# Rope products behind the score maxima on VectorE, and their sum behind the norm of the probabilities on GpSimd

## The reference

```python
q_c = layernorm(x) @ W_dq;  kv_c = ctx @ W_kvc
q_nope, q_rope = q_c @ W_uq, rope(q_c @ W_qr)          # 16 heads of 128 and of 64
k_nope, v, k_rope = kv_c @ W_uk, kv_c @ W_uv, rope(kv_c @ W_kr)
scores = (q_nope . k_nope + q_rope . k_rope) / sqrt(192)
scores = where(key in [seg - 8, seg], scores, -1e30)
x = x + (softmax(scores) @ v) @ W_o
# then: layernorm, gate, the two best of 8 experts per token, mean of their relu outputs, added to x
# rope(x): [x1 * cos - x2 * sin, x1 * sin + x2 * cos]
```

## Time and profile before

| | |
|---|---|
| median of 3 runs | 398.65 us (397.29 to 399.25) |
| the profiled execution | 397.97 us, span from the first to the last instruction 396.0 us |
| busy in the span: TensorE, VectorE, ScalarE, GpSimd | 84%, 69%, 63%, 58% |
| mean granted clock of TensorE | 0.984 |

### The profile page before, as it was taken

The page is one execution under the profiler, slowest core; times in us unless marked ns, Lnnn a source line. Parts: engine busy times, 40 slices in busy tenths (PEclk is TensorE's granted clock), DMA queues, the critical chain, the costliest instruction groups (busy, mean ns, idle before and its releaser), DMA issues.

```text
span 396.0 us, 9935 instructions
## 1 busy us (share of the span) xinstructions
PE 333.5 (84%) x2451; PEld 277.1 (70%) x2451; DVE 274.9 (69%) x1299; ACT 247.5 (63%) x843; POOL 227.8 (58%) x287
## 2 busy tenths in 40 slices
PE   0868999999879898988989898898988988799870
PEld 0656778777667777776777777777766767799750
DVE  2164878577688767778876877887677668756266
ACT  1232866888876777677677767767778635456440
POOL 4067646466975757576576757657655414677700
PEclk9999899999999999999999999999999999999995
DMA  8962711126121212132121213212221025566178
GB/s 288 343 250 83 266 55 55 55 71 171 55 81 56 81 61 99 53 103 83 53 80 67 92 53 106 80 53 80 80 82 54 2 68 156 173 198 190 50 256 293
DMA packets 28788, 45.29 MB, mean 114 GB/s; under 512 B 4428, under 2 KB 20191, under 8 KB 28112
## 3 DMA queue, kind: packets, MB, share of 16 engines
q1 hardware_dynamic: 25104, 37.30, 28.8%
q0 software_dynamic: 2960, 6.94, 4.9%
q10 hardware_dynamic: 688, 0.64, 0.6%
HBM read 26.46 MB, written 19.30 MB: 116 GB/s over the span
## 4 chain that ended last, share of the span: by engine, by line
issue 26%; PE 24%; POOL 23%; DVE 14%; DMA 5%; ACT 4%; POOLq 2%; DVEq 1%; ACTq 0%
POOL prob L1401 9%; PE psum L1163 4%; POOL slots L1421 4%; PE psum L681 3%; PE psum L1149 3%; PE psum L683 3%; PE psum L682 3%; DMA wcat<-in_w_kvc 2%; DVE nsc L1696 2%; POOL rope_c L1396 2%; DMA halves<-jout,jidx 2%; ACT prob L1257 2%; DVE x_all L1577 2%; POOL m_after L1378 1%; POOL mask L1386 1%
## 5 line engine op out<-in xcount | busy, mean ns | idle before, releaser
L1257 ACT ACTIVATE prob<-nsc,nmax 128x128 f32<-128x128 f32 x256 | 100.7, 395 | 62.7 <-DVE nmax L1696 62.7
L1401 POOL TENSOR_TENSOR prob<-prob,prec 128x512 f32<-128x512 f32 x64 | 67.2, 1050 | 27.3 <-DVE prec L1678 27.1
L1396 POOL TENSOR_TENSOR rope_c<-rope_c,rope_s 128x512 f32<-128x512 f32 x32 | 42.0, 1313 | 58.4 <-DVE rope_s L1672 58.3
L1696 DVE CUSTOM_DVE_ANT_0 nsc<-psum,mask 128x128 f32<-128x128 f32 x256 | 58.7, 285 | 18.7 <-PE psum L1163 13.3
L1163 PE MATMUL psum<-kT_all,qT 128*128 (+1 forms) x512 | 67.7, 275 | 1.2 <-DMA qT<-turned 1.2
L1163 PEld LDWEIGHTS psum<-kT_all,qT 128*128 128x128 f32 x512 | 62.2, 192 | 1.4 <-DMA qT<-turned 1.4
L1149 PE MATMUL psum<-ident,prob 128*128 128x128 f32 x256 | 41.8, 286 | 22.3 <-POOL prob L1401 22.3
L1149 PEld LDWEIGHTS psum<-ident,prob 128*128 128x128 f32 x256 | 26.9, 140 | 44.2 <-POOL prob L1401 36.3
L1257 ACT ACTIVATION_READ_ACCUMULATOR prob<-nsc,nmax 128x1 f32 x256 | 48.2, 188 | 0.0
L681 PE MATMUL psum<-qc_hi,wq_hi 96*128 96x256 f32 x128 | 41.6, 325 | 2.2 <-ACT qT L1300 0.9
L1443 POOL DMA_INDIRECT halves<-jout,jidx x33 | 32.8, 994 | 17.0 <-issue 6.8
(11 more groups left out here) (204 smaller groups left out, 821.1 us busy)
## 6 DMA issues: line engine op xcount, KB each, us to landing
turned<-rope_c SPq DMA_DIRECT2D x32, 256.0 KB, 2.0
qT<-turned SPq DMA_DIRECT2D x64, 128.0 KB, 2.4
wanted<-slots SPq DMA_DIRECT2D x33, 129.0 KB, 2.4
wo_raw<-in_w_o SPq DMA_DIRECT2D x2, 1024.0 KB, 15.9
we_raw<-in_expert_w SPq DMA_DIRECT2D x1, 2048.0 KB, 7.8
half<-halves SPq DMA_DIRECT2D x4, 512.0 KB, 7.1
x_all<-in_x SPq DMA_DIRECT2D x2, 640.0 KB, 18.4
slots<-pad_row SPq DMA_DIRECT2D x8, 129.0 KB, 3.7
```

The source lines that it names most:

```text
L1257: e = act.activation(prob[r][:, h, :], nsc[r][:, h, :], ACT.Exp, bias=nmax[r][:, h:h + 1], scale=-1.0, accum_out=psum_h[r][:, h:h + 1])
L1396: pool.tensor_tensor(into[:], into[:], rope_s[:], ALU.add).then_inc(m["rope_joined"], 1)
L1401: pool.tensor_tensor(p[:], p[:], prec[1 - r][:, :].unsqueeze(2).to_broadcast([P, HG, P]), ALU.mult).then_inc(m["prob_normed"], 1)
L1696: e = dve.tensor_tensor_reduce(nsc[r][:, h, :], B_S[r][:, h, :], mask[t][:], -SCALE, BIG, ALU.add, ALU.min, nmax[r][:, h:h + 1])
```

## The change

In even slots VectorE issues the two rope products, with their waits, behind the score maxima of the slot and no longer ahead of the reciprocal; GpSimd issues the norm of the probabilities first and the sum of the rope parts behind it. Nothing else moves, and no instruction is added or left out.

```diff
@@ GpSimd, slot(b, k)
+                if live(i - 1, GROUPS):
+
+                    at_least(pool, "recip_done", i)
+                    p = prob[1 - r]
+                    pool.tensor_tensor(p[:], p[:], prec[1 - r][:, :].unsqueeze(2).to_broadcast([P, HG, P]),
+                                       ALU.mult).then_inc(m["prob_normed"], 1)
                 if k % TPB == 0 and live(pn, QUADS):
                     into = rope_c[(k // TPB) % 2]
                     at_least(pool, "rope_parts", pn + 1)
                     pool.tensor_tensor(into[:], into[:], rope_s[:], ALU.add).then_inc(m["rope_joined"], 1)
-                if live(i - 1, GROUPS):
-
-                    at_least(pool, "recip_done", i)
-                    p = prob[1 - r]
-                    pool.tensor_tensor(p[:], p[:], prec[1 - r][:, :].unsqueeze(2).to_broadcast([P, HG, P]),
-                                       ALU.mult).then_inc(m["prob_normed"], 1)
@@ VectorE, slot(b, k), ahead of the reciprocal
-                if t == 0 and live(p + 2, QUADS):
-
-                    into = (k // TPB) % 2
-                    if isinstance(i, int) and i == -4:
-                        dve.wait_ge(S("ld_ropeq"), 16)
-                    at_least(dve, "qr_done", p + 3)
-                    at_least(dve, f"qr_out{into}", 16 * ((SLOTS // TPB // 2) * b + (k // TPB + 2) // 2))
-                    at_least(dve, "rope_joined", p + 2)
-                    a = B_R.rearrange("p (a n) -> p a n", a=2)
-                    dve.tensor_tensor(rope_c[into][:], a, ropeT[:, 0:1, :].to_broadcast([P, 2, L]), ALU.mult)
-                    dve.tensor_tensor(rope_s[:], a[:, ::-1, :], ropeT[:, 1:3, :], ALU.mult).then_inc(m["rope_parts"], 1)
...
@@ VectorE, slot(b, k), behind the score maxima
+                if t == 0 and live(p + 2, QUADS):
...
+                    dve.tensor_tensor(rope_c[into][:], a, ropeT[:, 0:1, :].to_broadcast([P, 2, L]), ALU.mult)
+                    dve.tensor_tensor(rope_s[:], a[:, ::-1, :], ropeT[:, 1:3, :], ALU.mult).then_inc(m["rope_parts"], 1)
```

More of the change, by code:

```diff
@@ L1392, in slot @@
                 nb, kn = b + k // SLOTS, k % SLOTS
[L1393 to L1396, removed]
                 if live(i - 1, GROUPS):
@@ L1402, in slot @@
                                        ALU.mult).then_inc(m["prob_normed"], 1)
+                if k % TPB == 0 and live(pn, QUADS):
+                    into = rope_c[(k // TPB) % 2]
+                    at_least(pool, "rope_parts", pn + 1)
+                    pool.tensor_tensor(into[:], into[:], rope_s[:], ALU.add).then_inc(m["rope_joined"], 1)
                 if kn == 0 and live(nb, B):
@@ L1699, in slot @@
                             e.then_inc(m["score_max"], 1)
+                if t == 0 and live(p + 2, QUADS):
+                    into = (k // TPB) % 2
+                    if isinstance(i, int) and i == -4:
+                        dve.wait_ge(S("ld_ropeq"), 16)
+                    at_least(dve, "qr_done", p + 3)
+                    at_least(dve, f"qr_out{into}", 16 * ((SLOTS // TPB // 2) * b + (k // TPB + 2) // 2))
+                    at_least(dve, "rope_joined", p + 2)
+                    a = B_R.rearrange("p (a n) -> p a n", a=2)
+                    dve.tensor_tensor(rope_c[into][:], a, ropeT[:, 0:1, :].to_broadcast([P, 2, L]), ALU.mult)
+                    dve.tensor_tensor(rope_s[:], a[:, ::-1, :], ropeT[:, 1:3, :], ALU.mult).then_inc(m["rope_parts"], 1)
                 if step == 1 and live(w, TILES) and not (isinstance(i, int) and i >= GROUPS):
```

## The result

The changed kernel takes 443.89 us (440.96 to 444.54, 4 runs) against 398.95 us (397.29 to 400.3, 4 runs): 1.1114 times the time before, 95% interval 1.1047 to 1.1181, or 44.9 us more. That is slower, as forecast, and 0.9 us above the upper end of the range (443). The profiled execution took 443.3 us; its span is 441.5 us.

What follows compares the result with a forecast made beforehand. GpSimd's order in slots with indirect DMAs (0, 1, 4, 5) was taken to set when TensorE's next slot opens. Waits of 27.5 us and 9.5 us of clock on 397.97, plus 0.7 for the median, gave 435 us, range 420 to 443.

Steps and rivals of the forecast that it cites:

- GpSimd's queue: Slots 0 and 4: mask, row copy, DMAs and next norm queue behind the sum waiting for late products; +2.13 and +2.21 us.
- Slots 0 to 2: Loop batch: the late sum delays mask, DMAs and slot 1's norm, so slot 2 opens 2.13 us later.
- slots 4 to 6: Loop batch: same delay on GpSimd, with no mask; slot 6 opens 2.21 us later.
- slots 2 to 4: VectorE: products now precede batch_sum, so slot 4 opens 0.62 us later, bounds 0 and 0.62.
- the 26.3 summed: Waits of batches with indirect DMAs, slot 0 six times, slot 4 five times: 6 x 2.75 + 5 x 1.96 us.
- the price of a low stretch: TensorE at 1.2 GHz behind the long waits before slots 2 and 6: 1.2 us each, between 0 and 1.5, eleven times.
- 3.7 hidden: Behind slot 2 the later TensorE hides VectorE's 0.62 us delay of batch_sum: -3.7 us in total.
- The rival whose clock holds (426): The loop's waits grow but TensorE's clock does not fall: 426 us at the median, chance 0.28.
- batches 0 and 1 at 0: Batches without indirect DMAs, where TensorE's own work is longer: no loss, between -1 and +1 us.
- the very first slot at 1.2: Products delay the key rows, for which TensorE waits until 37.30: 1.2 us, between 0 and 1.2.
- Faster: Rival: early norm removes the odd slots' waits, 1.18 us a batch; 391.5 us, chance 0.04.
- Moves nothing: Rival: slot 1's norm is not what TensorE needs next, so the delay lies in slack; 398.65 us, chance 0.03.

Runs made afterwards that it cites:

- warm: Changed kernel plus 13 unread TensorE products of 512 columns at the end of slots 1 and 5, from slot 16 on: 428.91 us, ratio 1.0762 to the kernel before.
- early_to12: The whole change only in slots before 12, the order of the kernel before from there on: 401.53 us, ratio 1.0101.
- early_only: The whole change only in slots before 16, the order of the kernel before from there on: 403.13 us, ratio 1.0149.
- late_only: The whole change only from slot 16 on, the order of the kernel before ahead of that: 439.75 us, ratio 1.1055.
- pool_only: Kernel before with only GpSimd's swap (norm first, rope sum second), VectorE's products in their old place: 397.29 us, ratio 0.9983.
- sum_next: Kernel before with GpSimd's rope sum moved behind the norm of the following odd slot, products in their old place: 389.18 us, ratio 0.9797.
- behind_recip: Changed kernel with VectorE's products directly behind the reciprocal, ahead of xT_lo and the score maxima: 401.82 us, ratio 1.0097 to the kernel before.
- dve_only: Kernel before with only VectorE's products moved behind the score maxima, GpSimd in the old order (sum, then norm): 510.57 us, ratio 1.2818.

## Why the prediction was right and where it was wrong

**GpSimd's queue: right.** Slots 0 to 2 were to grow by 2.13 us and grew by 2.05 (11.69 against 9.64 before); slots 4 to 6 by 2.21, and grew by 2.12 (11.17 against 9.05). The idle time before the sum is named after the products, and the odd slots no longer wait, as the prediction said. For slots 2 to 4 it gave 0.62, the place of batch_sum behind the products: with the clock held, in `warm`, the stretch grows by 0.58 (165.19 to 174.21, 9.02 us, against 8.44: from 187.94 to 196.38, where slot 4 starts in the same timeline). From slot 16 to slot 60 `warm` takes 217.08 us in its trace against 190.41 before, 26.7 more (two low stretches of its own are in it), against the 26.3 summed.

**The clock: mechanism right, size too small.** This is the first failed step: the price of a low stretch, taken as 1.2 us with 1.5 as its bound, eleven times, less 3.7 hidden, together 9.5. Measured: some 15.0, and batches of 42.2 and 42.9 us from slot 2 to slot 2 (167.14 to 209.34 to 252.25) where the prediction had 40 to 41. Compared with `warm` (3.62 us for slot 2 and for slot 6), slot 2 of the six batches took 10.8 us more in total and slot 6 of five batches 9.9 more: 20.7 us over eleven, 1.9 each. The bound of 1.5 came from a stretch of 3.00 us, but those are not the whole low stretch; in the half microsecond behind them the clock is still low:

```profile
41.50:42.00 0.50, 0.50 (x5) 0.50 (x4) 0.43 (x4) 0.50 (x2) 0.47 (x1) 0.57 0.18 33
```

So the one low stretch that I priced lasted about 3.4 us, worth 1.7. In the changed kernel the seven slots with such a stretch took 1.4 to 1.6 us more than in `warm`, and the four with twice its length 2.2 to 2.8; that a stretch can last so long I did not foresee. My reason for staying below the bound, that some of it passes while TensorE still waits, holds for only a small part: by the estimate above some 6 of 51 us of low clock. What came back behind these slots is at most 20.7 - 15.0 = 5.7 us. By the Trainium skill, TensorE: Matmul & The Clock Gate, section "HAM oscillation — how this bites in real kernels", each burst behind a long wait restarts at the lower clock; the runs agree, eleven long waits and eleven slow slots. The rival whose clock holds (426) is what `warm` measures, at 428.91.

**Start and batches 0 and 1: too small.** The second failed step: batches 0 and 1 at 0 and the very first slot at 1.2. Measured 3.2 us (`early_to12`) to 5.6 (`early_only`); within the whole change it is the difference to `late_only`, 44.9 - 41.4 = 3.5. The first slot the traces do not settle: its key rows come 1.51 us late in `early_to12` and 0.78 in the changed kernel, but 0.74 also in `pool_only` (38.04), where no product moved. Missed was that slots 8 and 10 of batch 1 have VectorE work for TensorE behind the products too; for slot 10 it is the very `batch_sum` and query halves that I priced at 0.62 in every later batch. A twelfth low stretch lies here as well, behind the wait of 2.33 us ahead of slot 16 (0.66 from 113 to 118); `early_to12`, which has no such wait, shows 1.00 from 111 to 118.

By differences the 44.9 us are 26.4 of waits (41.4 - 15.0), 15.0 of clock and 3.5 of start; they add up because each is a difference, so the sum is no check. The prediction had 26.3 + 9.5 + 1.2 = 37.0. The upper end of the range took 16.5 for the clock with nothing hidden, which is more than the 15.0 measured net; it was passed because the start stood in it at 1.2.

**The rivals.** "Faster" was to win if the sum could start by the end of the early norm; it starts 2.25 us later, held by the products that the score maxima precede. Its condition would not have been enough: in `pool_only` the sum does start at the end of the norm, the waits before the odd slots do go, and the time stays at 397.29, because they come back before slots 2 and 6. "Moves nothing" fell with the two long waits. Both were rightly small.

What stays open is why the clock falls early in one wait and late in another of the same length (3.38 us ahead of 145.72, where the slot loses 2.6 us; 3.34 ahead of 188.93, where it loses 1.6); it was not tried.

## What to carry to other kernels

A step that waits on another engine makes everything behind it in its queue wait too, so before moving it later, list that queue up to the next item the bounding engine needs: here two DMA issues and a norm, and 26 us. Put the waiting step behind the item that is needed, as `sum_next` does, and not only behind the one that is ready. When the new waits of TensorE are longer than those it already has, price the clock from rows with waits at least as long as the new ones and read the low stretch to its end; where there is no such row, take a wide upper bound. And search the written-out first batches for the same queues as the loop.

## What the runs showed of the hardware

- Added, useless work made the kernel faster by 15.0 us: 13 products of 512 columns in each of the eleven long waits held the granted clock at 0.98 from 118 to 330 us, where the changed kernel has 0.89.
- Of the eleven low stretches behind waits of 2.4 to 3.7 us in the changed kernel seven lasted about 3.4 us; the four before which the clock had fallen 0.8 to 2.0 us ahead of the work lasted about 6.8 (both estimated from half-microsecond stretches). The longer ones made their slot 2.2 to 2.8 us longer, the shorter ones 1.4 to 1.6.
- The length of the wait does not decide alone whether the clock falls. In `behind_recip` it fell behind waits of 1.80 us (ahead of 191.31) and 1.83 us (ahead of 296.77) and not behind four others of 1.56 to 1.81; in `pool_only` it fell behind a wait of 2.28 us (ahead of 153.16) and not behind others of 1.79 to 2.01. Behind two of five waits of 1.3 us for `oT_lo` in `warm` it fell too (0.68 from 132 to 136, 0.58 from 290 to 293). The kernel before has a wait of 1.58 us ahead of 118.54 and shows 1.00 behind it. First `behind_recip`, then `pool_only`:

```profile
191.00:195.00 4.00, 3.69 (x20) 3.63 (x21) 3.31 (x14) 1.77 (x8) 3.62 (x6) 0.60 0.07 24
```

```profile
153.00:157.00 4.00, 3.84 (x22) 3.78 (x23) 1.21 (x11) 1.45 (x5) 3.62 (x6) 0.61 0.04 15
```

- In `dve_only` a cast on VectorE took four times its usual 0.27 us while GpSimd's norm ran (205.88 to 206.92), and so in each batch of the loop:

```profile
205.88 1.04 POOL L1401 TENSOR_TENSOR prob<-prob,prec 128x512 f32<-128x512 f32 x1
...
206.00 1.07 DVE L1649 CAST qc_hi<-qc_all 96x256 fp32r x1
```

  The Trainium skill, SBUF — State Buffer, section "Who interferes with whom", says that a cast on VectorE can need the ports it shares with GpSimd and then stands until GpSimd's instruction ends. The row agrees: the cast ends 0.15 us behind the norm.
